# The first phase's norms on ScalarE, the row maxima out of its tail, the last chunk by halves

## The reference, cut to what matters

```python
x = x + 0.5 * ffn(layernorm(x))       # h = relu(x Wfc^T)^2, y = h Wproj^T; five steps of a spiking neuron on y, mean of the spikes
x = x + attention(layernorm(x))       # 16 heads of 16, rope on q and k, causal softmax, output projection
x = x + 0.5 * ffn(layernorm(x))
```

## Time and profile before

| what | us |
|---|---|
| median of three executions | 1399.8 |
| the profiled execution, its own time | 1402.6 |
| its span, first to last instruction | 1400.8 |
| TensorE busy in it | 1284.7 (92%) |
| VectorE busy | 1145.8 (82%) |
| ScalarE busy | 858.5 (61%) |
| GpSimd busy | 227.2 (16%) |

### The profile page before, as it was taken

The page is one execution under the profiler, slowest core; times in us unless marked ns, Lnnn a source line. Parts: engine busy times, 40 slices in busy tenths (PEclk is TensorE's granted clock), DMA queues, the critical chain, the costliest instruction groups (busy, mean ns, idle before and its releaser), DMA issues.

```text
span 1400.8 us, 22187 instructions
## 1 busy us (share of the span) xinstructions
PE 1284.7 (92%) x8224; PEld 779.2 (56%) x8224; DVE 1145.8 (82%) x2638; ACT 858.5 (61%) x1157; POOL 227.2 (16%) x205
## 2 busy tenths in 40 slices
PE   4999999966799999999999999999999989999996
PEld 3888888844444444444444444444444435888886
DVE  6578888887689899999999899989999953677875
ACT  4655555511067676776777677767766777656654
POOL 4003222342220020110110110200101021001000
PEclk9999999966679999999999999999999999999999
DMA  3124444863165080260440710800701131344312
GB/s 114 52 68 143 143 143 128 170 208 99 46 120 71 2 130 10 35 97 10 70 63 10 109 24 10 124 16 17 116 9 37 50 91 47 83 132 138 93 46 75
DMA packets 88740, 110.30 MB, mean 79 GB/s; under 512 B 25308, under 2 KB 60892, under 8 KB 87004
## 3 DMA queue, kind: packets, MB, share of 16 engines
q1 hardware_dynamic: 88632, 108.88, 33.5%
HBM read 64.62 MB, written 42.21 MB: 76 GB/s over the span
## 4 chain that ended last, share of the span: by engine, by line
PE 70%; DVE 20%; ACT 6%; issue 3%; DMA 0%; DVEq 0%; POOL 0%; ACTq 0%; SPq 0%
PE m_ps L1092 19%; PE o_ps L1129 17%; DVE maxes L1029 9%; PE s_ps L1113 6%; PE ups_a L610 6%; PE yps_c L627 5%; PE yps_a L627 5%; PE ups_c L610 4%; PE gps_a L658 4%; DVE masked L1032 3%; ACT probs L1008 3%; DVE xmv_a L392 2%; PE gps_c L643 2%; PE tps_a L636 1%; PE gps_a L643 1%
## 5 line engine op out<-in xcount | busy, mean ns | idle before, releaser
L1008 ACT ACTIVATE probs<-s_ps 128x1024 f32<-128x1024 f32 (+3 forms) x640 | 538.9, 897 | 224.0 <-PE s_ps L1113 223.1
L1029 DVE TENSOR_REDUCE maxes<-m_ps 128x1 f32<-128x512 f32 x768 | 489.4, 683 | 46.4 <-PE m_ps L1092 45.1
L1092 PE MATMUL m_ps<-kT,qT 64*128 64x512 f32 (+3 forms) x1280 | 453.5, 456 | 42.5 <-DVE maxes L1029 17.1
L1092 PEld LDWEIGHTS m_ps<-kT,qT 64*128 64x128 f32 x1280 | 205.2, 188 | 387.3 <-DVE maxes L1029 261.4
L1113 PE MATMUL s_ps<-qT,kT 64*128 64x512 f32 (+3 forms) x1280 | 309.9, 393 | 6.9 <-ACT probs L1008 6.5
L1129 PE MATMUL o_ps<-probs,v_w 128*32 128x512 f32 (+3 forms) x2560 | 306.2, 551 | 0.6 <-POOL probs L977 0.2
L1032 DVE CUSTOM_DVE_ANT_0 masked<-m_ps,mask 128x128 f32<-128x128 f32 (+3 forms) x512 | 235.8, 486 | 44.3 <-PE m_ps L1092 38.8
L977 POOL TENSOR_SCALAR_AFFINE_SELECT probs<-probs 128x512 f32<-128x512 f32 x128 | 82.2, 642 | 674.1 <-ACT probs L1008 674.1
L1113 PEld LDWEIGHTS s_ps<-qT,kT 64*128 64x128 f32 x1280 | 167.3, 189 | 31.6 <-ACT probs L1008 29.3
L1129 PEld LDWEIGHTS o_ps<-probs,v_w 128*32 128x32 f32 x2560 | 50.8, 108 | 73.3 <-issue 56.8
L506 DVE TENSOR_TENSOR h_lo_c<-hsq_c,h_hi_c 128x512 fp32r<-128x512 f32 x64 | 46.1, 722 | 53.3 <-ACT h_hi_c L343 28.9
(11 more groups left out here) (124 smaller groups left out, 1889.1 us busy)
## 6 DMA issues: line engine op xcount, KB each, us to landing
qT<-qkT_parts SPq DMA_DIRECT2D x96, 128.0 KB
kT<-qkT_parts SPq DMA_DIRECT2D x48, 256.0 KB
qkT_parts<-qk_hi_a SPq DMA_DIRECT2D x32, 256.0 KB, 4.6
qkT_parts<-qk_lo_a SPq DMA_DIRECT2D x32, 256.0 KB, 4.8
sumsT<-osum SPq DMA_DIRECT2D x32, 256.0 KB, 2.4
table_a<-in_rot SPq DMA_DIRECT2D x8, 768.0 KB, 7.7
xin_a<-in_x SPq DMA_DIRECT2D x8, 512.0 KB, 3.6
xres_a<-in_x SPq DMA_DIRECT2D x8, 512.0 KB, 5.0
```

The source lines that it names most:

```text
L1008: act.activation(probs[:, b % PBUF, 2 * hp:2 * hp + 2, off:CH], s_ps[hp][:, :, off:CH], ACT.Exp, scale=D ** -0.5).then_inc(exp_done, 1)
L1029: dve.tensor_reduce(out, m_ps[:, i % MB, 0:width], AX.X, ALU.max).then_inc(max_read, 1)
L1092: pe.matmul(m_ps[:, i % MB, 0:width], qT[n % 2][r0:r0 + HR, j, hp, t * P:(t + 1) * P], kT[n % 2][r0:r0 + HR, hp, k * CH:k * CH + width], s ...
```

## The change

Six edits, in the diff's order. **SP's queue**, second phase: `load_attn` and `load_x` move one slot earlier, behind `store_recip` at f = 7; the last chunk's output is stored in two halves, and its x2 is neither stored nor read back. **Norms**: in the first phase they are ScalarE's, as x * rstd + offset, mid at f = 3 and pre at f = 4, with one more small VectorE instruction for the offset; in the second phase they stay on VectorE in another form (tensor_scalar). At the start, std and norm of chunk 0 stand ahead of the weights' splits on ScalarE and VectorE, the third weight's split is later, and GpSimd's memsets wait for the first norm. **y by banks**, second phase: y is copied in two halves, each when its `down` matmuls have ended, and the next chunk's `down` waits for each half alone. **Last chunk by halves**: its three last `down` slots run for tiles 0 and 1 and then for tiles 2 and 3, comparisons and sum too. **`add_bias`** moves from f = 1 to f = 5 and waits for the norm. **Units**: `slot_of` gives the first phase only four slots, f = 0..3 of iteration 10, and `place_units` spreads group 0's 160 units over these and its blocks 0 to 19. By the listing's arithmetic the four lead slots hold 8, 10, 7 and 8 units (33), and blocks 0 to 19 hold 127 instead of 76, seven or eight in most; the shift of j = 1 comes at the end of block 2 (its scores start in block 4), that of j = 2 in block 10 (its scores start in block 12). The other groups are placed as before.

```diff
+        wait(sp, "sum_done", c + 1 + half)
+        sp.dma_start(rows(dst, c)[:, T // 2 * half:T // 2 * (half + 1), :], xb[:, T // 2 * half:T // 2 * (half + 1), :])\
+          .then_inc(s["sum_out"], 16)
...
         elif f == 0:
+            if it == 0:
+                load_attn(2)
+                load_x(2)
+            if it == NC + 1:
+                store_half(it - 2, 0)
+                store_half(it - 2, 1)
+            elif has(it, 2):
+                store_sum(it - 2)
+            if has(it, 1) and it < NC:
+                load_rest(it - 1)
             if has(it, -2):
-                load_attn(it + 2)
-                load_x(it + 2)
-            if has(it, 2):
-                store_sum(it - 2)
-            if has(it, 1):
-                load_rest(it - 1)
-            if has(it, -1):
                 store_x2(it + 1)
             if has(it, -3):
                 load_denom(it + 3)
         elif f == FC - 1 and has(it, -3):
             store_recip(it + 3)
+            load_attn(it + 3)
+            load_x(it + 3)
...
+    def norm(which, c, q, x, o, c0):
+        wait(act, "offset", q + 1)
+        wait(act, which + "_T", c)
+        for t in range(T):
+            last = act.activation(o[:, t, :], x[:, t, :], ACT.Identity, bias=ln[:, 4, c0 + t:c0 + t + 1],
+                                  scale=ln[:, 3, c0 + t:c0 + t + 1])
+        last.then_inc(s[which + "_norm"], 1)
...
+            wait(act, "one", 1)
+            act.activation(ln[:, 4, 0:1], ln[:, 5, 0:1], ACT.Sqrt)
+            std(0)
+            norm("pre", 0, 0, xin, xn, 0)
             take_weight(0)
-            std(0)
             high("pre", 0, xT_hi)
             take_weight(1)
-            take_weight(2)
         elif x == 18:
...
-        if f == LAG and has(it, 1):
+        if not first and f == LAG and has(it, 1):
+            wait(act, "spike", STEPS * (it - 1))
+            for half in range(2):
+                if half == 0:
+                    wait(act, "half_done", it)
+                else:
+                    wait(act, "down_done", FC * it)
+                act.activation(y[:, CH * half:CH * (half + 1)],
+                               yps[:, T // 2 * half:T // 2 * (half + 1), :].rearrange("p t e -> p (t e)"), ACT.Copy)\
+                    .then_inc(s["y_evac"], 1)
...
+        if first and f == 3 and has(it, 2):
+            norm("mid", it - 2, it + 1, xsum, xm, T)
+        if first and f == 4 and has(it, -1):
+            norm("pre", it + 1, it + 1, xin, xn, 0)
+        if first and (it, f) == (0, 6):
+            take_weight(2)
...
+        if first:
+            wait(dve, "pre_norm", min(q, NC))
...
+        if first:
+            wait(dve, "rstd", q + 1)
+            dve.scalar_tensor_tensor(out=l[:, 4, :], in0=mv[:, lo:hi, 0], scalar=-1.0, in1=l[:, 3, :],
+                                     op0=ALU.mult, op1=ALU.mult).then_inc(s["offset"], 1)
...
         wait(dve, which + "_T", c)
         for t in range(T):
-            last = dve.scalar_tensor_tensor(out=o[:, t, :], in0=x[:, t, :], scalar=mv[:, c0 + t, 0:1],
-                                            in1=ln[:, 3, c0 + t:c0 + t + 1].broadcast_to([P, E]),
-                                            op0=ALU.subtract, op1=ALU.mult)
+            last = dve.tensor_scalar(o[:, t, :], x[:, t, :], mv[:, c0 + t, 0:1], ln[:, 3, c0 + t:c0 + t + 1],
+                                     ALU.subtract, ALU.mult)
...
+    def last_sum(c, half):
+        cols, tiles = slice(CH * half, CH * (half + 1)), slice(T // 2 * half, T // 2 * (half + 1))
+        wait(dve, "y_evac", 2 * c + 1 + half)
+        if half == 0:
+            wait(dve, "sum_done", c)
+            wait(dve, "x2_done", c + 1)
+        done = STEPS * (c + half)
+        dve.tensor_scalar(count[:, cols], y[:, cols], LEVELS[0], None, ALU.is_ge).then_inc(s["spike"], 1)
+        for k in range(1, STEPS):
+            wait(dve, "spike", done + k)
+            dve.scalar_tensor_tensor(out=count[:, cols], in0=y[:, cols], scalar=LEVELS[k], in1=count[:, cols],
+                                     op0=ALU.is_ge, op1=ALU.add).then_inc(s["spike"], 1)
+        wait(dve, "spike", done + STEPS)
+        dve.scalar_tensor_tensor(out=xb[:, tiles, :].rearrange("p t e -> p (t e)"), in0=count[:, cols],
+                                 scalar=0.5 / STEPS, in1=x2[:, tiles, :].rearrange("p t e -> p (t e)"),
                                  op0=ALU.mult, op1=ALU.add).then_inc(s["sum_done"], 1)
...
     def lead(x=None):
         if first:
+            dve.memset(ln[:, 5, 0:1], 1.0).then_inc(s["one"], 1)
             wait(dve, "x_in", 16)
             norm_stats(xin, 0)
             norm_var(0)
+            norm_scale(0)
             split_low(0)
-            norm_scale(0)
-            norm("pre", 0, 0, xin, xn, 0)
             low("pre", 0, xT_hi, xT_lo)
             split_low(1)
-            split_low(2)
         elif x in (6, 8, 14):
...
             h_low(it, f)
-        if first and f == 3:
-            if has(it, 2):
-                norm("mid", it - 2, it + 1, xsum, xm, T)
-            if has(it, -1):
-                norm("pre", it + 1, it + 1, xin, xn, 0)
-        if f >= LAG and has(it, 1):
+        if first and (it, f) == (1, 4):
+            split_low(2)
+        if not first and it == NC and f == LAG:
+            last_sum(it - 1, 0)
+            last_sum(it - 1, 1)
+        elif f >= LAG and has(it, 1) and (first or it < NC):
             spikes(it - 1, f - LAG)
-        if f == 0 and has(it, 2):
+        if f == 0 and has(it, 2) and (first or it <= NC):
...
-        if not first and f == 1 and has(it, -2):
+        if not first and f == 5 and has(it, -2):
+            wait(pool, "pre_norm", it + 2)
...
         if f == 0:
-            wait(pe, "y_evac", it)
...
         for t in range(T):
+            if not first and f == 0 and t == T // 2:
+                wait(pe, "y_evac", 2 * it)
             for i, (wt, h) in enumerate(((down_hi, h_hi), (down_lo, h_hi), (down_hi, h_lo))):
                 last = pe.matmul(yps[:, t, :], h[:, f % HB, t * P:(t + 1) * P], wt[:, f, :],
                                  start=(f == 0 and i == 0 and t % 2 == 0), stop=(f == FC - 1 and i == 2),
                                  skip_group_check=True)
+            if not first and f == FC - 1 and t == T // 2 - 1:
+                last.then_inc(s["half_done"], 1)
         last.then_inc(s["down_done"], 1)
+    def last_downs(it):
+        for half in range(2):
+            for f in range(FC - LAG, FC):
+                wait(pe, "lo_done", it * FC + f + 1)
+                for t in range(T // 2 * half, T // 2 * (half + 1)):
+                    for i, (wt, h) in enumerate(((down_hi, h_hi), (down_lo, h_hi), (down_hi, h_lo))):
+                        last = pe.matmul(yps[:, t, :], h[:, f % HB, t * P:(t + 1) * P], wt[:, f, :], start=False,
+                                         stop=(f == FC - 1 and i == 2), skip_group_check=True)
+                if half == 1:
+                    last.then_inc(s["down_done"], 1)
+            if half == 0:
+                last.then_inc(s["half_done"], 1)
...
-        if has(it, k):
+        if not first and it == NC and f < LAG:
+            if f == 0:
+                last_downs(it - 1)
+        elif has(it, k):
...
-def place_units():
+def place_units(first):
 room = []
-for g in range(MAX_FROM, MAX_TO):
+for g in range(first, MAX_TO):
     j, b = [(j, b) for j in range(NJ) for b in range(T * j + T)][g % BLOCKS]
-    room.append(1 + T - max(0, b - T * j))
+    room.append(1 + T if first == -LEAD and g < 0 else 1 + T - max(0, b - T * j))
 cost = [u[5] + 110 for u in UNITS]
...
-unit_slots, order = place_units(), []
+unit_slots, order = [place_units(MAX_FROM if n else -LEAD) for n in range(GROUPS)], []
 for g in range(MAX_FROM, LAST):
     for n in range(GROUPS):
-        order += [(g, ("unit", n, u)) for u in unit_slots.get(g - BLOCKS * n, [])]
+        order += [(g, ("unit", n, u)) for u in unit_slots[n].get(g - BLOCKS * n, [])]
 for n in range(GROUPS):
...
     def slot_of(it, f):
-        return FC * (it - NC - 3) + f
+        return f - LEAD if it == NC + 2 and f < LEAD else None
...
         b_lead, b_first_values, b_slot = middle[3](pool)
         c_lead, c_body = second[3](pool)
+        pool.wait_ge(a_s["pre_norm"], 1)
         b_lead()
```

More of the change, by code:

```diff
@@ L255, in body @@
                 store_recip(it + 3)
+                load_attn(it + 3)
+                load_x(it + 3)
         def end():
-            wait(sp, "sum_out", 16 * NC)
+            wait(sp, "sum_out", 16 * (NC if first else NC + 1))
             if first:
@@ L420, in spikes @@
             if k == 0:
-                wait(dve, "y_evac", c + 1)
+                wait(dve, "y_evac", c + 1 if first else 2 * (c + 1))
                 wait(dve, "sum_done", c)
@@ L616, in down @@
             if f == 0:
-                wait(pe, "y_evac", it)
+                wait(pe, "y_evac", it if first else 2 * it - 1)
                 if first and it == 0:
```

(2 more changed lines are left out.)

19 lines of the change are left out of this document (13 added, 6 removed).

## The result

The kernel after takes 1392.46 us (median of 20 runs, 1385.72 to 1398.06), the kernel before 1401.37 (20 runs beside them, 1396.86 to 1409.8). The ratio is 0.9934, 95% interval 0.9918 to 0.995: faster by 0.7%, where the forecast of 1374 was 1.9% and its range ended at 1388. The profiled execution took 1390.95 us, its span is 1389.2 and its mean granted clock 0.95 (before 1402.6, 1400.8 and 0.96).

What follows compares the result with a forecast made beforehand. TensorE bounds the first phases, TensorE and VectorE nearly fill the attention, the tail is a handover chain. -6.2 - 7.9 - 33 + 29 - 5.0 - 1.5 - 1.3 = -25.9: 1376.7 profiled, 1374 us as median, range 1361 to 1388.

Steps and rivals of the forecast that it cites:

- The start: Chunk 0's norm and weight splits: first `up` starts at 15.8 us instead of 22.05, -6.2 us.
- Steady first phase: Mid norm on ScalarE: TensorE's waits for it in five chunks all go, -7.9 us, between -9 and -3.
- The tail: Chunks 5 to 7 and lead slots: first exponential at 356 us instead of 389, -33 us.
- Blocks 0 to 19: Group 0's attention with 51 units more: 75.8 us against 49.6, late shifts besides; +29 us, between +21 and +36.
- a low clock for six blocks at most: Upper bound for blocks 0 to 19: 83 us, if VectorE is as full as now and the clock low.
- rival 1: Blocks 0 to 19 at half clock, VectorE setting the pace: +45 over 16 blocks, 1419 us, slower; 4%.
- The shifts: Two late shifts in blocks 0 to 19, taken at 1.5 and 2 us.
- Second phase and end: Waits for y -5.0 us, first chunk -1.5, last chunk by halves -1.3.
- a threshold of ten blocks: In blocks 0 to 19: half clock decides the result from ten blocks of 6.8 us instead of 3.8 on.
- the move itself: Units moved from the tail into blocks 0 to 19: -33 us in the tail, +29 in the blocks.
- Rival 2: Handovers hold the tail, late shifts queue behind group 1's loads: tail -25, shifts +8, 1386.5 us, still faster; 22%.
- The test that the forecast named for itself: Forecast wrong if the tail keeps over 85 us, blocks 0 to 19 take over 86, or clock there below 0.8.

Runs made afterwards that it cites:

- e16: e1 without GpSimd's wait for the first norm, so its memsets run from 0.8 us again; 1379.75 us, ratio 0.9843.
- e15: e1 with the first phase's mid norm on VectorE again at f = 3, in the tensor_scalar form; 1383.88 us, ratio 0.9872.
- e1: The kernel after with group 0's units placed as before, all other edits kept; 1373.54 us, ratio 0.9812.
- e11: The kernel of e1 run once more, unchanged; 1374.25 us, ratio 0.9791.
- e5: The kernel after without the stores of group 0's shifts of j = 1 and 2 into qT; 1380.82 us, ratio 0.9853.
- e4: The kernel after with group 1's loads five slots later on SP's queue, behind the shift of j = 2; 1389.65 us, ratio 0.9917.
- e14: e1 with GpSimd's add_bias of the second phase at f = 1 again, without the wait for the norm; 1378.97 us, ratio 0.9837.
- e2: The kernel before with the units' move alone; 1415.37 us, ratio 1.0101.
- e8: e5 with a second, 256-column matmul ahead of each unit's in blocks 0 to 19 of group 0; 1383.91 us, ratio 0.9845.
- e13: e5 with each maximum in blocks 0 to 19 of group 0 over at most 256 columns; 1356.06 us, ratio 0.9676.
- e3: The kernel after with each maximum in blocks 0 to 19 of group 0 over at most 256 columns; 1382.81 us, ratio 0.9867.

## Why the prediction was wrong, step by step

- **The start**, -6.2: -6.5 (15.53 against 22.05). Right; e16 shows that most of it is the wait of the memsets. The working had that only in taking every small operation at its short duration, and named no cause.
- **Steady first phase**, -7.9: -8.1. Right, and caused by the edit (e15: 6.5 us of waits come back). A norm on ScalarE takes 2.07 us where 2.0 was taken.
- **The tail**, -33, 74 us to the first exponential: 74.2. Right in its length; that all of it is the units' is not, as some 3 to 5 us are the other edits' (e1, e11).
- **Blocks 0 to 19**, +29, and the step that failed: **+48.4**, above its bound of +36. The price was VectorE's: 68.8 us of work, 75.8 with small operations and gaps. VectorE's work is right, 69.8 us, and at 2.4 GHz its pace too: in e5's stretches at full clock it is busy 93 to 96%, so 69.2 us of work would take 69.2 / 0.945 = 73.2. What was wrong is the sentence that bounded the term with a low clock for six blocks at most, and, in rival 1, that TensorE still has work for 90% of the time. It had, and the clock fell. From 73.2 the working goes on: 14.4 us for the clock (to e5's 87.6), then 10.4 for the shifts and what follows from them, which makes 98.0. The shifts were taken at 3.5 us and stalled TensorE for 7.2: 2.34 ahead of block 4, 4.84 ahead of block 12, where group 1's loads stand before the stores (e4). The term's own parts add up to 26.2 + 3.5 = 29.7 and not 29, which changes nothing.
- **Second phase and end**, -5.0, -1.5, -1.3, in all -7.8: -8.5. Of the 8.5, 4.5 are `add_bias`'s place (e14). Per chunk it is 27.0 us instead of 27.7, in the first 26.5 instead of 29.0 (-2.5 instead of -1.5), and from the last `down` to the last instruction 10.0 instead of 11.5.

So one term is off by more than a microsecond, and it is the whole miss: the others are together 1 us better than forecast, the blocks 19.4 worse. The profiled execution stands 14.3 us above the 1376.7 forecast for it, as the stretch behind block 20 gave back some 4; by the ratio of the medians it is 17.

**The rivals.** Rival 1, half clock through the blocks, is what happened, and was given 4%. Its mechanism was described rightly and then priced at its extreme: 6.8 us for each block, +45 against the forecast, with a threshold of ten blocks. Some twelve blocks did run at half clock, most or all of the way, but 6.8 is the price of the longest of them (block 6 took 6.76, the shortest 4.6), and the mean over blocks 4 to 19 was 5.2. So the blocks lost 19 us against the forecast instead of 45, and the kernel was still faster as a whole. It owes that to the other terms: the move itself, forecast as a gain of 4 us, is a loss of 14 (e2) to 21 (e1) by the traces. A rival with so high a price looks unlikely; between it and the forecast lay all the cases in which the clock comes and goes, and they had no chance of their own. The range ended 14 us above the forecast. Rival 2's late shifts came true too. The Trainium skill's rule ("TensorE: Matmul & The Clock Gate", What's actually happening), that the throttle is the default and activity releases it, agrees with e8 and e13, where TensorE's denser work kept 2.4 GHz. Alone it does not account for e5, where 23.61 us of work in 23.9 did not bring 2.4 GHz back. It had been read as a small risk; it was the largest term.

The test that the forecast named for itself, blocks over 86 us or a clock below 0.8, was met on both counts: 98.0 and 0.62.

## What to carry to other kernels

Before moving work into a stage that is nearly balanced, ask which engine will set the pace at full clock. If it is not TensorE, work out the stage a second time with TensorE at 1.2 GHz: here a stage of 73 us by VectorE is 88 us with the clock coming and going. The fastest kernels here moved 13 or 20 units and not 51; against moving none they are some 4 us ahead, which is not clear of the noise. A small store that a later stage waits for is better put ahead of bulk loads in its queue (4.84 us of waiting behind them, 2.11 ahead, e4), and making the blocks faster can make that store later (e3). By the trace e4's change of order is worth 2.7 us of waiting, by the medians it is within the noise.
